# Attention after a first mixture-of-experts stage: GpSimd adds up the exponentials of eight of 12 and ten of 16 key tiles in the third and fourth block, instead of five and seven

## The reference

```python
x = x + 0.5 * ffn(layernorm(x), ...)      # 8 experts, 2 chosen per token
x = x + attn(layernorm(x), wq, wk, wv, wo)
x = x + 0.5 * ffn(layernorm(x), ...)
# attn: 16 query heads of 32, 4 key heads (each for 4 query heads), rotary embedding
attn = einsum('bhqd,bhkd->bhqk', q, k) / sqrt(32)
attn = where(mask, -inf, attn)            # causal
attn = softmax(attn, axis=-1)
out = einsum('bhqk,bhkd->bhqd', attn, v)  # then @ wo
```

## Time and profile before

| | |
|---|---|
| Profiled execution, its own time | 1382.4 us |
| Its span | 1381.1 us |
| TensorE busy | 1221.9 us, 88% |
| VectorE busy | 884.9 us, 64% |
| ScalarE busy | 661.7 us, 48% |
| GpSimd busy | 551.0 us, 40% |
| Mean granted TensorE clock | 0.958 of full speed |
| Scores, line 1493 | 640 matmuls, 248.5 us |
| Weighings, line 1505 | 1280, 152.5 us |
| Sums, line 1518 | 896, 96.7 us |
| Exponentials, line 1597 | 640, 305.6 us |
| Links, line 1651 | 160 (128 and 32), of some 1.28 us |
| Masks, line 1636 | 64, 40.9 us |

### The profile page before, as it was taken

How to read it: one execution, slowest core, us unless ns; L and a number is a source line. 1 busy time by engine, 2 the same in 40 slices (tenths; PEclk the granted TensorE clock), 3 DMA queues, 4 the chain that set the end, 5 groups by cost and what they waited for, 6 DMA issues and landing times.

```text
span 1381.1 us, 22056 instructions
## 1 busy us (share of the span) xinstructions
PE 1221.9 (88%) x7484; PEld 784.2 (57%) x7484; DVE 884.9 (64%) x2056; ACT 661.7 (48%) x1313; POOL 551.0 (40%) x458
## 2 busy tenths in 40 slices
PE   4499999679888999999989999999999849988884
PEld 4478888557775554454445455454433347766663
DVE  7867777479996665666676675667620375655662
ACT  2545555335455543454355454465567524444441
POOL 5635444223110110013344454527458653444443
PEclk8689999889999999999999999999999969999998
DMA  9723333355540021042013003023000343555554
GB/s 333 312 92 107 107 109 110 110 136 96 89 67 32 2 63 32 32 93 32 32 62 63 2 1 124 1 93 62 2 1 1 133 184 84 91 90 93 90 89 61
DMA packets 56891, 114.42 MB, mean 83 GB/s; under 512 B 7664, under 2 KB 17136, under 8 KB 56752
## 3 DMA queue, kind: packets, MB, share of 16 engines
q0 software_dynamic: 26112, 68.17, 22.5%
q1 hardware_dynamic: 30672, 44.85, 9.6%
HBM read 79.71 MB, written 33.55 MB: 82 GB/s over the span
## 4 chain that ended last, share of the span: by engine, by line
PE 57%; DMA 19%; DVE 14%; issue 5%; ACT 4%; SPq 1%; POOL 0%; POOLq 0%; DVEq 0%; ACTq 0%
DMA out<-Y,DI 13%; PE bank L1493 10%; PE bank L1505 10%; PE bank L797 8%; PE bank L952 8%; PE bank L1518 5%; PE bank L820 4%; PE bank L1555 3%; DVE PM L965 3%; DMA XA<-y 2%; DVE bank L967 2%; PE bank L779 1%; ACT P L1597 1%; PE bank L1535 1%; PE bank L1313 1%
## 5 line engine op out<-in xcount | busy, mean ns | idle before, releaser
L1597 ACT ACTIVATE P<-bank 128x512 f32<-128x512 f32 (+3 forms) x640 | 305.6, 536 | 299.6 <-PE bank L1493 295.5
L965 DVE TENSOR_REDUCE PM<-bank 128x1 f32<-128x512 f32 x384 | 252.8, 685 | 100.6 <-PE bank L952 99.6
L1493 PE MATMUL bank<-Qs,Ks 98*128 98x512 f32 (+3 forms) x640 | 248.5, 413 | 8.0 <-ACT P L1597 6.3
L952 PE MATMUL bank<-Ks,Qs 96*128 96x512 f32 (+3 forms) x640 | 238.9, 392 | 8.8 <-DVE PM L965 5.3
L1493 PEld LDWEIGHTS bank<-Qs,Ks 98*128 98x128 f32 x640 | 117.6, 190 | 151.3 <-issue 86.0
L1651 POOL TENSOR_TENSOR CH<-CH,P 128x512 f32<-128x512 f32 x128 | 160.3, 1286 | 71.9 <-ACT P L1597 71.0
L1636 POOL TENSOR_SCALAR_AFFINE_SELECT P<-P 128x512 f32<-128x512 f32 x64 | 40.9, 638 | 308.5 <-ACT P L1597 308.5
L967 DVE CUSTOM_DVE_ANT_0 bank<-bank,KB 128x128 f32<-128x128 f32 (+3 forms) x256 | 124.7, 497 | 57.8 <-PE bank L952 57.0
L952 PEld LDWEIGHTS bank<-Ks,Qs 96*128 96x128 f32 x640 | 121.9, 191 | 63.0 <-DVE PM L965 32.2
L1505 PE MATMUL bank<-P,V 128*32 128x512 f32 (+3 forms) x1280 | 152.5, 548 | 0.2 <-POOL P L1636 0.2
L908 DVE TENSOR_TENSOR DL<-W,DH 128x512 fp32r<-128x512 f32 x152 | 98.4, 689 | 46.4 <-ACT DH L869 33.7
(11 more groups left out here) (184 smaller groups left out, 1903.3 us busy)
## 6 DMA issues: line engine op xcount, KB each, us to landing
xn<-XN SPq DMA_DIRECT2D x8, 1024.0 KB, 6.7
WR<-L_ffn_w POOLq DMA_DIRECT2D x16, 512.0 KB, 15.5
XO<-y POOLq DMA_DIRECT2D x8, 1024.0 KB, 9.6
WR<-L_ffn_w SPq DMA_DIRECT2D x16, 512.0 KB, 7.6
XA<-y POOLq DMA_DIRECT2D x24, 256.0 KB, 4.2
W<-L_ffn_w POOLq DMA_DIRECT2D x8, 512.0 KB, 25.0
XA<-L_attn_x SPq DMA_DIRECT2D x16, 256.0 KB, 3.4
XO<-L_attn_x SPq DMA_DIRECT2D x4, 1024.0 KB, 7.9
```

Of the source, the lines that this page charges most:

```text
L952: pe.matmul(bk(g, bank)[:, 0:n], g.Qs[b][0:96, G % 4 * 4 + h, c * P:c * P + P], g.Ks[0:96, G % 4, k * BQ:k * BQ + n], start=True, stop=Tru ...
L965: dve.tensor_reduce(dst, bk(g, bank)[:, 0:n], AX.X, ALU.max).then_inc(s(f"free{bank}"), 1)
L1493: pe.matmul(bk(g, i % 3)[:, o:BQ], g.Ks[0:98, G % 4, k * P:k * P + P], g.Qs[G // 4][0:98, G % 4 * 4 + j, o:BQ], start=True, stop=True).the ...
L1597: act.activation(a.P4[buffer_of(n)][:, j, o:BQ], bk(g, i % 3)[:, o:BQ], ACT.Exp, scale=scale).then_inc(s("exp"), 1)
```

## The change

`ADDED` has other tiles: 0, 1, 2, 4, 5, 7, 8, 9 in the third block and 0, 1, 2, 4, 5, 6, 8, 9, 10, 12 in the fourth. Tiles 8 and 9 of the third and tile 12 of the fourth lie on the diagonal. A link of such a tile waits for the mask (which is on the same engine), and the additions take only the columns from `first(b, k)` on, 384 for tile 9 of the third block and 512 for all others. Sums: in the third block the tiles left to TensorE are 3, 6, 10 and 11 (before 2, 5 and 7 to 11), in the fourth 3, 7, 11, 13, 14 and 15 (before 2, 5, 8 and 10 to 15).

```diff
-ADDED = ((), (), (0, 1, 3, 4, 6), (0, 1, 3, 4, 6, 7, 9))
+ADDED = ((), (), (0, 1, 2, 4, 5, 7, 8, 9), (0, 1, 2, 4, 5, 6, 8, 9, 10, 12))
...
+        if n in MASKED:
+            pool.wait_ge(s("mask"), MASKED[n] + 1)
+        o = first(b, k)
         for h in range(4):
             pool.wait_ge(s("exp"), 4 * n + h + 1)
-            ins = pool.tensor_tensor(to[:, h, :], two[:, h, :], one[:, h, :], ALU.add)
+            ins = pool.tensor_tensor(to[:, h, o:BQ], two[:, h, o:BQ], one[:, h, o:BQ], ALU.add)
         ins.then_inc(s("link"), 1)
```

## The result

The changed kernel takes 1423.53 us (median of four runs, 1423.29 to 1425.85). Over the kernel before the ratio is 1.0319, 95% interval 1.0294 to 1.0344: 43.7 us slower, where 20 were forecast. The time lies above the stated range (1385 to 1414). The sign, the place and the waits were right; the size was not.

The account below looks back on a forecast made before the run. TensorE was taken to bound both blocks. Waits of 33.6 us less 19.8 of sums gave +13.9; plus 7.4 for the clock, less 1 of old VectorE waits, +20: 1400 us, range 1385 to 1414.

Parts of the forecast that it names:

- TensorE sets the pace, 19.8 us of sums: Third and fourth blocks: TensorE is the bottleneck, so the sums taken from it save 19.8 us.
- The narrow link, 3.79 us: Third block, tile 9: GpSimd's 384-wide link takes 3.79 us, four pieces at 3/4 of a full link's 5.05.
- Mask 8 to mask 10, 10.76 us: Third block, GpSimd: 10.76 us from the start of mask 8 to the end of mask 10, links between.
- group 15, 46.7 us: Last group, GpSimd: nine links, 45.45 us, and two masks, 1.28, without a gap, need 46.7 us.
- Waits for masks, 33.6 us: Both blocks: TensorE's weighings wait for late masks, 19.3 us in the third and 14.3 in the fourth.
- Waits less sums, +13.9: Both blocks: 33.6 us of new waits less 19.8 us of saved sums make the run 13.9 us longer.
- The clock, 7.4 us: TensorE's clock falls near six waits, 1.65 us each, 9.9 in all; three quarters counted, 7.4 us.
- a stretch at the lower clock lasts 3.3 us here: Both blocks: each fall of TensorE's clock lasts 3.3 us, all busy, and costs 1.65 us.
- the six places that the forecast names: The waits of groups 8, 9, 10, 11, 14 and 15, where TensorE's clock was expected to fall.
- The rival that doubled the stretch: Six places keep the low clock for two stretches, 19.8 us instead of 7.4: about +32, 1412 us; chance 0.13.
- About 1 us of old waits for VectorE: About 1 us of TensorE's old waits for VectorE goes, since VectorE catches up while TensorE waits.
- all else at nothing: Every other effect, such as a link's wait for its mask and the OT and SM copies, costs nothing.

Follow-up runs that it names:

- the reductions: The changed kernel with VectorE's small copy (line 984) and subtraction (986) written as three reductions: 1412.2 us (1.0216).
- both remedies: The changed kernel with matmuls of zeros before the weighings that wait for masks, and VectorE's small copy and subtraction as three reductions: 1393.7 us (1.0094).

## Why the prediction was right in kind and wrong in size

- *TensorE sets the pace, 19.8 us of sums.* Right: 19.6 with the sums gone and nothing else changed.
- *The narrow link, 3.79 us.* Right: 3.8 us from the start of the link to the next mask in group 11, so 0.95 us a piece.
- *Mask 8 to mask 10, 10.76 us; group 15, 46.7 us.* Right: 10.9 and 46.7.
- *Waits for masks, 33.6 us.* Right within a fifth: 27.3 in the changed kernel, and 30.2 with the reductions. A part of group 15's shows as a wait for an exponential (1.4 us), as forecast; why the rest is less was not taken apart.
- *Waits less sums, +13.9.* Right: +13.4 with both remedies. That it is so near is in part luck, since the zero matmuls are only about as long as the waits.
- *The clock, 7.4 us.* This term was mis-sized. Filling the waits for masks took 17.3 us off by the medians (1423.5 to 1406.3) and 21 by the ratios. The slow clock in all made TensorE's work 28.9 us longer than in the kernel with the sums alone gone, a part of it behind waits for VectorE. The step that failed is "a stretch at the lower clock lasts 3.3 us here": that was the length of both falls before, behind idle pieces of 1.2 us and less, and it was taken for falls behind waits of 1.5 to 4.6 us. At the six places that the forecast names, the clock was down for 65 us in the two blocks instead of 6 x 3.3 = 20; with VectorE's waits it was some 88 us, where it had been 9. The rival that doubled the stretch went the right way, and not far enough. What sets the length of such a stretch stays open: behind one wait of 2.8 us it was 3.3 us in one kernel and 13.6 in another. The trace before had a long one too, outside the two blocks and with TensorE mostly idle in it, which the forecast left out:

```profile
1107.50:1131.00 23.50, 9.86 (x89) 8.03 (x88) 17.25 (x55) 6.84 (x8) 13.02 (x3) 0.50 0.65 239
```

- *"About 1 us of old waits for VectorE" to be gained, all else at nothing.* Wrong in sign. The waits for the tops grew from 3.3 to 8.6 us, and copy and subtraction behind them cost 11.4 us by the medians (14 by the ratios) with the falls of the clock that they set off. This is the second step that failed, a cost put at nothing. I had not looked at what VectorE does from SBUF while GpSimd adds; the trace before had a hint, one copy at 0.85 us, against a median of 0.18.

The sum closes within the scatter. By the medians, taken on different chips: 13.4 left with both remedies, 17.3 for the clock at the masks, 11.4 for the copy, 42.1 of 43.7. By the ratios, each against the kernel before on its own chip: 13, 21 and 14, 48 of 44, so that the two remedies may overlap by some 5 us. How much of the copy's part is its own wait and how much the clock behind it was not taken apart.

## What to carry to other kernels

Work moved to an idle engine is priced by its place in that engine's queue: ask what stands behind it that the bottleneck waits for, and at what time. A wait of TensorE can cost more than its length, since the clock can fall with it; here filling 27 us of waits with useless matmuls made the kernel 17 us faster or more, and TensorE work put into a wait was free. Even with the waits for masks gone the added links took some 16 us of the 20 that the sums gave: work on an idle engine is not free when others wait for its buffers, or are slowed while it works. Before GpSimd gets more element-wise work, list the small SBUF copies and two-source operations of VectorE in that stretch; a reduction can do some of them.

## What the runs showed of the hardware that I had not expected

A VectorE copy of 128x16 took 4.45 us instead of 0.18 while GpSimd's additions ran, as long as what was left of four of them; other such copies were held for one addition, 1.30 us at most. As a reduction it took 0.18 us in the same place. The lower clock lasted 3.3 us behind one wait of 2.8 us and 13.6 us behind another of the same length, with TensorE busy for 12.2 of the 13.6. Removing 19.6 us of TensorE work from a kernel whose TensorE then waits brought nothing (1423.5 us against 1419.4 with the work left in).
